# One kernel of eight layers: layer 2's attention with its output weights folded into its values, and a first stage that looks one tile further ahead

## The reference

```python
xn = _layernorm(x, ln_gamma, ln_beta)
q = (xn @ w_q).reshape(B, SQ, NUM_HEADS, DIM_HEAD)        # 16 heads of 64
k, v = jnp.split(context @ w_kv, 2, axis=-1)              # 77 context rows
attn = jax.nn.softmax(einsum('bqhd,bkhd->bhqk', q * SCALE, k), axis=-1)
out = einsum('bhqk,bkhd->bqhd', attn, v).reshape(B, SQ, INNER)
out = (out @ w_out + b_out) * tanh(gate[0])
```

## Time and profile before

| | us |
|---|---|
| median of three runs | 1280.36 |
| the profiled execution | 1276.38 |
| its span, first to last instruction | 1274.5 |
| TensorE busy in the span | 1113.6 (87%) |
| VectorE busy | 811.4 (64%) |
| ScalarE busy | 495.3 (39%) |
| GpSimd busy | 178.0 (14%) |
| mean granted TensorE clock | 0.956 of full speed |

### The profile page before, as it was taken

How to read it: one execution, slowest core, us unless ns; L and a number is a source line. 1 busy time by engine, 2 the same in 40 slices (tenths; PEclk the granted TensorE clock), 3 DMA queues, 4 the chain that set the end, 5 groups by cost and what they waited for, 6 DMA issues and landing times. The chain is left out here.

```text
span 1274.5 us, 19932 instructions
## 1 busy us (share of the span) xinstructions
PE 1113.6 (87%) x6672; PEld 936.5 (73%) x6672; DVE 811.4 (64%) x1848; ACT 495.3 (39%) x946; POOL 178.0 (14%) x234
## 2 busy tenths in 40 slices
PE   4685799988999699979999986899967999989996
PEld 3553476667888588869888864888846887878886
DVE  5758899986776455267676646777636554565443
ACT  3544543334444454532333311455524432323231
POOL 2212000001112322220000012022114000010000
PEclk9877899998999799999999999999979999999998
DMA  9212010001000000000000022000002111111212
GB/s 289 52 30 56 1 11 0 1 1 66 2 0 1 1 1 1 1 1 1 0 0 0 1 102 108 1 1 0 1 2 83 50 60 56 54 49 49 65 61 75
DMA packets 35289, 42.42 MB, mean 33 GB/s; under 512 B 18533, under 2 KB 24495, under 8 KB 34332
## 3 DMA queue, kind: packets, MB, share of 16 engines
q1 hardware_dynamic: 34355, 40.90, 10.1%
q10 hardware_dynamic: 873, 0.72, 0.2%
HBM read 38.43 MB, written 3.17 MB: 33 GB/s over the span
## 5 line engine op out<-in xcount | busy, mean ns | idle before, releaser
L340 PE MATMUL psum<-ident,work 128*128 128x128 f32 (+1 forms) x976 | 164.9, 287 | 64.4 <-DVE work L307 20.9
L351 ACT COPY work<-psum 128x256 f32<-128x256 f32 (+2 forms) x304 | 128.8, 447 | 222.3 <-PE psum L340 213.1
L302 POOL TENSOR_TENSOR rstd<-ve,mhalf 128x1 f32<-128x1 f32 x128 | 83.6, 654 | 847.5 <-DVE ve L297 847.5
L340 PEld LDWEIGHTS psum<-ident,work 128*128 128x128 f32 (+1 forms) x976 | 115.1, 146 | 104.0 <-DVE work L307 24.8
L1121 PEld LDWEIGHTS psum<-zone,work 128*128 128x128 f32 x1024 | 123.6, 192 | 3.5
L1121 PE MATMUL psum<-zone,work 128*128 (+5 forms) x1024 | 124.9, 278 | 0.0
L1867 DVE TENSOR_TENSOR work<-psum,work 128x512 f32<-128x512 f32 x68 | 46.9, 690 | 101.5 <-ACT work L1804 101.4
L1247 DVE TENSOR_REDUCE small<-psum 128x6 f32<-128x462 f32 x144 | 83.5, 580 | 26.4 <-PE psum L1079 14.9
L1323 PE MATMUL psum<-early,work 128*128 128x352 f32 x256 | 85.7, 488 | 8.8 <-ACT zone L478 4.0
L1737 PE MATMUL psum<-x_hi,ew_hi 128*128 128x512 f32 (+1 forms) x272 | 87.2, 402 | 2.6 <-ACT work L1804 2.6
L1248 DVE TENSOR_TENSOR work<-psum,small 128x462 f32<-128x462 f32 x144 | 84.3, 586 | 4.9
(11 more groups left out here) (239 smaller groups left out, 2442.8 us busy)
## 6 DMA issues: line engine op xcount, KB each, us to landing
work<-expert_shares SPq DMA_DIRECT2D x64, 256.0 KB, 3.1
early<-in_experts_in SPq DMA_DIRECT2D x1, 6528.0 KB, 18.6
x<-in_x_in SPq DMA_DIRECT2D x4, 512.0 KB, 6.8
early<-in_W_in SPq DMA_DIRECT2D x2, 1024.0 KB, 6.0
out_x<-x SPq DMA_DIRECT2D x1, 2048.0 KB, 7.5
early<-in_Wk SPq DMA_DIRECT2D x1, 1024.0 KB, 6.2
early<-in_Wq SPq DMA_DIRECT2D x1, 1024.0 KB, 8.8
zone<-in_Wv SPq DMA_DIRECT2D x1, 1024.0 KB, 13.1
```

What stands on the lines that cost most here:

```text
L302: pool.tensor_tensor(rstd[:, slot:slot + 1], ve[:, slot:slot + 1], mhalf[:, 0:1], ALU.pow).then_inc(s["rstd_ready"], 1)
L340: last = pe.transpose(dst[0:rows, at:at + n], src, ident[0:n, 0:n])
L351: act.copy(dst, src).then_inc(s["tr_copied"], 1)
```

## The change

**Layer 2's attention** gets functions of its own, `att2_tensor`, `att2_scalar` and `att2_vector`. Values times output weights are formed beforehand (`VO`, 20 blocks of 128 head-and-row pairs x 256 columns), so probabilities times `VO` is the projected output: ten f32 products of 256 columns and one bias a tile. VectorE only takes the negated maximum of each bank; ScalarE computes `exp(score - max)` head by head, straight from PSUM with the maximum as bias: 16 instructions of 77 columns. VectorE then sums, inverts and multiplies in SBUF, and the probabilities are turned after that. A tile passes through two steps of TensorE. The normalised x has a bank of its own and is looked at one step further ahead.

**Preparing VO.** In the first stage the values are computed turned (8 units of two products of 154 columns, steps 14 to 16) and stored masked, into areas that GpSimd sets to zero first (5120 words of each partition). In `ffn0_*`, steps 4 to 13, two units a step fold them with the output weights: 34 f32 products of 256 columns in all, and 20 copies. The trip of layer 2's values through DRAM, the split of its output weights and its `value_blocks` on GpSimd go away.

**The first stage** turns tile t+2 in step t and computes the scores of t+1 ahead of the output of t-1 and of the setup units; VectorE normalises t+3 and takes statistics of t+4, and adds the residual of t-2. Folded keys are spread over steps 10 to 14. What concerns layer 2's feed-forward matrix and the router (`misc_first`, `misc_pool`, `misc_last`, `product_ab`, `turn_router`) moves into `ffn1_*`, with its DMAs.

**Loops.** `pipeline` without counts writes all steps out; `ffn0_*` on TensorE and ScalarE is now written so.

```diff
 def pipeline(eng, first, step, counts=(), last=T, ahead=2):
+    if not counts:
+        for s in range(first, last + 1):
+            step(s, s % 2)
...
-        def project_wide_values(pe, dst, bb, c):
+        def project_wide_values(pe, dst, t):
             for k in range(KD):
...
+                last = pe.matmul(dst[:, 0:B * SK], scratch[2]["Wv"][:, k, t * P:(t + 1) * P], ctxT[:, k, :],
+                                 start=k == 0, stop=k == KD - 1)
             return last
+        def take_wide_values(act, src, t):
+            values = by_batch(src[:, 0:B * SK])
+            for j in range(2):
+                cols = slice((2 * t + j) * SK, (2 * t + j + 1) * SK)
+                into = ((v_even[:, :, cols], values),) if t % 2 == 0 else tuple(
+                    (v_odd[bb][:, cols], values[:, bb, :]) for bb in range(B))
+                for dst, part in into:
+                    last = act.activation(dst, part, ACT.Identity, scale=hmask[64][:, j:j + 1])
+            return last
+        VO_FIRST, VO_UNITS = 4, 2
...
+        def fold_values(pe, dst, bb, k):
+            a, z = k * P, (k + 1) * P
+            pairs = range(a // (2 * SK), min(7, (z - 1) // (2 * SK)) + 1)
+            for t in pairs:
+                v = v_even[:, bb, a:z] if t % 2 == 0 else v_odd[bb][:, a:z]
+                last = pe.matmul(dst[:, 0:D], v, Wo[2][:, t, :], start=t == pairs[0], stop=t == pairs[-1])
+            return last
+        def take_folded_values(act, src, bb, k):
+            return act.copy(VO[:, bb * KT + k, :], src[:, 0:D])
...
+        FOLDS = {10: 2, 11: 3, 12: 4, 13: 4, 14: 3}
+        VALUES = {14: 1, 15: 4, 16: 3}
+        TURNED_UNITS = 4 + 8 + 1 + 8 + 4
...
-            for t in range(-1, T + 1):
+            xn_unit = 0
+            for t in range(-2, T + 1):
...
-                if has(t):
-                    pe.wait_ge(s["tr_copied"], tr.n)
-                    wait(pe, s["exp_done"], t - 1)
-                    for k in range(KD):
-                        last = pe.matmul(bank[p][:, 0:SK], xnT[p][:, k, :],
-                                         ctxT[:, k, (t // TB) * SK:(t // TB) * SK + SK], start=k == 0, stop=k == 1)
-                    last.then_inc(s["s_ready"], 1)
                 if has(t - 1):
                     pe.wait_ge(s["exp_done"], t)
                     transposes(pe, s, tr, [(pr0[1 - p], SK)], TR34)
                     pt_unit = tr.n
...
+                if has(t + 2):
+                    pe.wait_ge(s["xn_ready"], t + 3)
+                    transposes(pe, s, tr, [(xn[p][:, k * P:(k + 1) * P], P) for k in range(KD)], TR34)
+                    xn_unit = tr.n
                 if has(t + 1):
-                    pe.wait_ge(s["xn_ready"], t + 2)
-                    transposes(pe, s, tr, [(xn[1 - p][:, k * P:(k + 1) * P], P) for k in range(KD)], TR34)
+                    pe.wait_ge(s["tr_copied"], last_xn)
+                    wait(pe, s["exp_done"], t)
+                    for k in range(KD):
+                        c = ((t + 1) // TB) * SK
+                        last = pe.matmul(bank[1 - p][:, 0:SK], xnT[1 - p][:, k, :], ctxT[:, k, c:c + SK],
+                                         start=k == 0, stop=k == 1)
+                    last.then_inc(s["s_ready"], 1)
                 if has(t - 1):
                     pe.wait_ge(s["tr_copied"], pt_unit)
                     wait(pe, s["y_read"], t - 2)
...
         def start_vector(dve):
-            s = a_s[0]
-            for t in range(-2, T + 1):
+            s, tr = a_s[0], Count()
+            for t in range(-4, T + 2):
...
                 if has(t):
                     dve.wait_ge(s["s_ready"], t + 1)
                     dve.tensor_reduce(small[:, p:p + 1], bank[p][:, 0:SK], AX_X, ALU.max,
                                       negate=True).then_inc(s["s_read"], 1)
-                if has(t + 1):
-                    ln_apply(dve, t + 1, 1 - p, s, xn[1 - p]).then_inc(s["xn_ready"], 1)
-                if has(t + 2):
...
+                if has(t + 3):
+                    wait(dve, s["tr_copied"], tr.n)
+                    ln_apply(dve, t + 3, 1 - p, s, xn[1 - p]).then_inc(s["xn_ready"], 1)
+                if has(t + 4):
...
+                    ln_stats(dve, t + 4, p, s)
...
                 if t >= 8:
                     value_blocks(pool, 1, t - 8)
-            misc_pool(pool)
+            pool.wait_ge(set_s["filled"], TURNED_UNITS)
+            pool.memset(v_even, 0.0).then_inc(set_s["vp_zero"], 1)
+            for v in v_odd:
+                pool.memset(v, 0.0).then_inc(set_s["vp_zero"], 1)
...
+        PT2_CHUNKS = [(0, 3), (3, 7), (7, 10)]
+        PT2_BANKS = (3, 4, 3)
...
+        def att2_tensor(pe):
...
+            def scores(t, p, j):
...
+                wait(pe, s["exp_done"], 3 * t - 2 + j)
+                n, col = (h1 - h0) * SK, (t // TB) * HK + h0 * SK
+                for i, (x_, a) in enumerate(three((xT_hi[p], xT_lo[p]), A2_PARTS)):
+                    for k in range(KD):
+                        last = pe.matmul(bank[j][:, 0:n], x_[:, k, :], a[k][0][:, bass.ds(col + a[k][1], n)],
+                                         start=i == 0 and k == 0, stop=i == 2 and k == KD - 1)
+                last.then_inc(s["s_ready"], 1)
+            def turn_probabilities(t, p, j):
...
+                pe.wait_ge(s["norm_done"], 3 * t + j + 1)
+                wait(pe, s["pt_copied"], 3 * t + (0, -1, 1)[j])
+                for k in range(c0, c1):
+                    last = pe.transpose(bank[PT2_BANKS[j]][:, (k - c0) * P:(k - c0 + 1) * P], prob[p][:, k * P:(k + 1) * P],
+                                        ident[:])
+                last.then_inc(s["pt_filled"], 1)
+            def outputs(t, p):
+                wait(pe, s["y_read"], t - 1)
...
+                for j, (c0, c1) in enumerate(PT2_CHUNKS):
+                    pe.wait_ge(s["pt_copied"], 3 * t + j + 1)
+                    for k in range(c0, c1):
+                        pe.matmul(bank[6 + p][:, 0:D], probT2[p][:, k, :], vo[:, bass.ds(v0 + k * D, D)],
+                                  start=k == 0, stop=False, skip_group_check=True)
+                pe.matmul(bank[6 + p][:, 0:D], ones3[:], brow[:, 2 * D:3 * D], start=False, stop=True,
+                          skip_group_check=True).then_inc(s["y_ready"], 1)
+            def step(t, p):
+                for j in range(3):
+                    if has(t):
...
+                        scores(t, p, j)
+                    if has(t - 1):
...
+                        turn_probabilities(t - 1, 1 - p, j)
+                if has(t + 1):
+                    pe.wait_ge(s["xn_ready"], t + 2)
...
+                    last.then_inc(s["x_filled"], 1)
+                if has(t - 1):
+                    outputs(t - 1, 1 - p)
...
+            end_stage(pe, "pe")
+        def att2_scalar(act):
...
+            def take_probabilities(t, p, j):
...
+                act.wait_ge(s["pt_filled"], 3 * t + j + 1)
+                act.copy(probT2[p][:, c0:c1, :], bank[PT2_BANKS[j]][:, 0:(c1 - c0) * P].rearrange("p (a b) -> p a b", a=c1 - c0)
+                         ).then_inc(s["pt_copied"], 1)
+            def exps(t, p, j):
...
+                act.wait_ge(s["max_done"], 3 * t + j + 1)
+                for h in range(h0, h1):
+                    last = act.activation(prob[p][:, h * SK:(h + 1) * SK], bank[j][:, (h - h0) * SK:(h - h0 + 1) * SK],
+                                          ACT.Exp, bias=nmx[:, h:h + 1])
+                last.then_inc(s["exp_done"], 1)
+            def step(t, p):
+                for j in range(3):
+                    if has(t - 1):
+                        take_probabilities(t - 1, 1 - p, j)
+                    if j == 2 and has(t + 1):
+                        act.wait_ge(s["x_filled"], t + 2)
...
+                    if has(t):
+                        exps(t, p, j)
...
+            end_stage(act, "act")
+        def att2_vector(dve):
...
+            def maximum(t, j):
...
+                dve.wait_ge(s["s_ready"], 3 * t + j + 1)
+                dve.tensor_reduce(nmx[:, h0:h1], heads(bank[j], j), AX_X, ALU.max,
+                                  negate=True).then_inc(s["max_done"], 1)
+            def normalise(t, p, j):
...
+                n = h1 - h0
+                pr = heads(prob[p][:, h0 * SK:h1 * SK], j)
+                dve.wait_ge(s["exp_done"], 3 * t + j + 1)
+                link(dve, dve.tensor_reduce(rs[:, h0:h1], pr, AX_X, ALU.add))
+                link(dve, dve.reciprocal(rs[:, h0:h1], rs[:, h0:h1]))
+                dve.tensor_tensor(pr, pr, rs[:, h0:h1, None].to_broadcast([P, n, SK]),
+                                  ALU.mult).then_inc(s["norm_done"], 1)
+            def step(t, p):
...
+                if has(t):
+                    maximum(t, 0)
...
+                if has(t):
+                    maximum(t, 1)
+                    normalise(t, p, 0)
+                    maximum(t, 2)
...
+                if has(t + 1):
```

(24 more changed lines are left out.)

374 lines of the change are left out of this document (186 added, 188 removed).

## The result

The changed kernel takes 1222.93 us (median of four runs, 1222.59 to 1223.46) against 1280.11; the ratio is 0.955, 95% interval 0.952 to 0.958. Forecast were 1223. The profiled execution took 1222.84, 53.5 less than the one of before. The total came out right, but its terms did not, so the stages have to be looked at one by one.

The account below looks back on a forecast made before the run. TensorE's instructions bound layer 2's attention; waits and chains set the first stage. Terms -49, -16, +6 and +1.5 sum to -57.5: 1276.38 becomes 1218.9, plus 3.98 for the median, 1223 us; range 1212 to 1234, chance 54%.

Parts of the forecast that it names:

- Layer 2: Layer 2's attention stage: fewer TensorE instructions a tile shorten it by 49 us (bounds -56 and -32).
- the pitch: Layer 2's attention: time from one tile's bias row to the next, forecast 9.75 us (bounds 9.3 and 10.9), 12.31 before.
- The loop of VectorE and ScalarE: Layer 2's attention: chain of maximum, exponentials, copies, split and normalising, 9.7 us a tile with seven handovers, level with TensorE.
- The first rival: Layer 2's attention: VectorE and ScalarE set the pace, exponentials 0.335 without overlap, 10.9 us a tile, 1240 us; 16%.
- First stage: First stage: shorter values, lookahead and int4 and router work leaving shorten it by 16 us (bounds -5 and -27).
- Lookahead: First stage: scores one tile ahead remove 40% of VectorE's 17.7 us of other waits for them, -7 us (0 to -17.7).
- values -7 and int4 work -2: First stage: layer 2's values shrink from 9.58 us of TensorE, -7 (-4 to -9.6); int4 and router work leaves, -2.
- The fill: First stage: GpSimd zeroing 5120 words a partition, 5.8 us, put at nothing; up to 5 us if ScalarE's copies wait.
- a rival: First stage: GpSimd's fill beside VectorE and the masked copies stand on the chain, stage only -5, 1234 us; 14%.
- Layer 0's feed-forward: Layer 0's feed-forward: folding makes ten steps 10.4 us against VectorE's 9.79, +6 us (0 to +14).
- Layer 1's feed-forward: Layer 1's feed-forward: layer 2's int4 product and router turning add 1.1 us of TensorE, +1.5 us (0 to +4).
- The signs that were named: Trace checks, such as first stage's end at 102 us; wrong if layer 2's stage exceeds 170 or another moves over 3.

Follow-up runs that it names:

- n_few_products: The changed kernel with seven of the ten products of a tile in layer 2's output left out; bias rows 8.1 to 8.2 us apart (9.13 in the changed kernel).

## Why the prediction was right, and where it was not

**The whole, 1223 forecast, 1222.93 measured: that it is so near is luck.** The stage terms add up to -57.5 and the profiled execution fell by 53.5. To this 1218.9 the forecast added 3.98, by which the median of the kernel before lies above its profiled execution. After, the profiled execution (1222.84) and the median are the same, so that the 3.98 had nothing to stand for and just filled the terms' error of 4.0. The terms err by 8.9, 6.2, 3.9 and 2.1 us, one one way and three the other.

**Layer 2, -49 forecast, -57.9 measured**, outside its own bounds of -56 and -32. The mechanism was right (n_few_products confirms it) and the edges of the stage too: first scores after 2.0 us (1.5 said), the second tile's 8.1 behind (8.4), the last tile's and what follows 15.75 (16.2). The term mis-sized is the pitch, 9.12 in the mean of 14 tiles (687.25 less 559.51) where 9.75 was said: 8.8 us in all. It lies below the lower bound of 9.3 too, and that bound does not follow from its terms, which give 9.5 (5.09, 4.3 and 0.12). Scores and turns take 4.77 for 5.09, the products 4.32 for 4.4, the bias 0.03 for 0.12, and of 0.15 for handovers nothing is seen.

**The loop of VectorE and ScalarE** was summed to 9.7 and called level with TensorE. It is 8.2. The chain is the one that was summed, but two of its terms were too large. The 12 exponentials, put at 3.4, hold it for 2.6 (from the first to the copy behind them 1.32 and 1.26), and for the seven handovers, put at 0.7, it shows some 0.3, ahead of the split, where VectorE's statistics stand. The first rival fell with it: exponentials in a row overlap and cost 0.215 each. The price that follows from the Trainium skill's "ScalarE: Activation LUTs", section "What ACT_TABLE_LOAD costs", is 251 ns with its overlap, an estimate; the measured one lies below it, and far below 335.

**First stage, -16 forecast, -9.8 measured.** Lookahead was put at -7 and gave -7.8 alone (-12 with the new values behind it). The step that failed is the next: values -7 and int4 work -2. These edits gave 2 to 3 behind the lookahead and cost 2 without it. Taking 9.58 us in one piece out of TensorE's queue was counted as nearly all gain. In the old order with ScalarE's zeros its step did become 7.0 us shorter; but the folded keys that moved ahead, and the values in the last three steps, took it back, and VectorE's waits for scores stayed at 25.8 us, only in other places. In the changed kernel, too, the stage's end is drawn out: from the last tile's maximum to the end it takes 13.2 us (94.98 to 108.17), 11.0 before. Which of the moved pieces costs what was not tested one by one. The fill was put at nothing because ScalarE's copies would not have to wait for it, and they did not; that it stands in VectorE's way, for 4.0 us, was left to a rival. (A smaller slip: a third off 4.2 leaves 2.8 and not 2.6.)

**Not foreseen**: the root behind GpSimd's waiting instruction, 8.7 us, of which a kernel gets back about 3.5. The prediction named GpSimd's roots as a chain, but did not ask what stands ahead of them in their queue. That is the question to put to every step of lookahead.

**Layer 0's feed-forward, +6 forecast, +9.9 measured.** A step was nearly right: L1400 (L1555 in the changed kernel) comes every 9.7 to 10.1 us where 10.4 was said. The terms given for it add up to 10.9, with two waits for banks of 0.46; the trace has none of these waits, and 8.5 and 1.5 alone give 10.0. The cover was not right: the sum took 9.79 as VectorE's pace in all ten steps. For the last two tiles it runs in 7.6, and there each fold costs in full; L1400 of the last two tiles came 7.57 and 7.59 apart before, 9.85 and 9.81 after. So of the 9.9 us 4.5 lie in these two steps, 2.7 in those ahead of them, 2.2 behind the last L1400 and 0.6 ahead of the first.

**Layer 1's feed-forward, +1.5 forecast, +3.6 measured.** Work was counted, 1.1 us of TensorE and VectorE's in its waits. That GpSimd's reduction would pile up ten splits behind it was not; the eight that ran in a row before (7.44 us) had doubled single instructions of VectorE at most (1.39 for 0.69), and ten in a row did more.

**The signs that were named.** Layer 2 ended at 153.6, well under 170, and of the stages for which nothing was forecast layer 1's attention moved by 0.4 and the last three together by 0.2. Of the finer signs the waits for scores (10 us or less, measured 1.6) and ScalarE's not waiting for the fill came true; the pitch of 9.75, exponentials 0.28 apart, the first stage's end at 102 and the 10.4 us of layer 0's steps did not.

## What to carry to other kernels

When a product chain leaves TensorE, the new pitch is TensorE's own instructions if the other engines' line, followed in the order in which they really run, is shorter: follow the chain instruction by instruction, at the prices that a row of instructions has in the trace and not at those of a single one. Each step of lookahead asks for its inputs one step earlier from every engine in the chain, so look in each in-order queue for an instruction that waits on a transfer ahead of the one now wanted. Work on GpSimd that has slack by its own times can still cost VectorE nearly its whole length (4.0 of the fill's 4.4 us here), and a gain of a few us in one stage must be read with the granted clock of the next, in more than one profile.
